# Fused transformer kernel: where in a turn of the first attention the score maxima are taken

## What is computed

```python
def _L0_attn_ref(x, W_Q, W_K, W_V, W_K_prime, W_O, alpha):    # 16 heads of 16, T = 384 rows an image
    scores = jnp.einsum('bhqd,bhkd->bhqk', q, k) / SCALE
    attn = jax.nn.softmax(scores, axis=-1)                     # the row maximum is subtracted
    out_std = jnp.einsum('bhqk,bhkd->bhqd', attn, v)
    scores_p = jnp.einsum('bhqd,bhkd->bhqk', q, kp) / SCALE
    attn_p = jax.nn.softmax(scores_p, axis=-1)
    out_p = jnp.einsum('bhqk,bhkd->bhqd', attn_p, v)
    out = alpha * out_std + (1.0 - alpha) * out_p
...
def fp4_quant_dequant(x):                                      # of w_gate, w_up and w_down too
    scale = jnp.max(jnp.abs(xb), axis=-1, keepdims=True) / 6.0
    scale = jnp.maximum(scale, jnp.float32(1e-12))
    idx = jnp.searchsorted(_MID, jnp.abs(xb / scale))
    q = _GRID[idx] * jnp.sign(xb) * scale
```

## Time and profile before

| | us |
|---|---|
| median of 3 runs | 1869.66 (1868.59 to 1869.83) |
| the profiled execution | 1862.18, its span 1860.4 |
| prologue ring, from about 74.4 | to 135.17, where turn 0 begins |
| turns 0 to 6 | 135.17 to 660.17, 75 on average |
| turn 7, then the wait for the weights | 660.17 to 718.29 |
| PE / DVE / ACT busy over the span | 94% / 54% / 36% |

### The profile page before, as it was taken

The page is one execution under the profiler, slowest core; times in us unless marked ns, Lnnn a source line. Parts: engine busy times, 40 slices in busy tenths (PEclk is TensorE's granted clock), DMA queues, the critical chain, the costliest instruction groups (busy, mean ns, idle before and its releaser), DMA issues. The chain is left out here.

```text
span 1860.4 us, 29106 instructions
## 1 busy us (share of the span) xinstructions
PE 1757.0 (94%) x9935; PEld 1118.6 (60%) x9935; DVE 1007.1 (54%) x2072; ACT 674.2 (36%) x1289; POOL 407.2 (22%) x415
## 2 busy tenths in 40 slices
PE   7989999899999987899989999997999999999997
PEld 3324444344444433677755656655676768999997
DVE  6597877778777877788874554442311111122221
ACT  2116655556566675455432332223111110111110
POOL 2101021120211001788831212110121211100100
PEclk9989999999999999999999999998999999999999
DMA  6832632525425111000056000000010003343311
GB/s 198 132 54 65 91 78 40 99 53 84 78 40 93 25 48 56 17 0 0 1 198 195 1 0 0 0 0 1 18 37 23 30 24 102 124 151 102 105 32 33
DMA packets 111955, 112.84 MB, mean 61 GB/s; under 512 B 11455, under 2 KB 104433, under 8 KB 111858
## 3 DMA queue, kind: packets, MB, share of 16 engines
q1 hardware_dynamic: 98610, 83.21, 20.1%
q10 hardware_dynamic: 9600, 18.92, 2.9%
q0 software_dynamic: 3648, 9.46, 1.4%
HBM read 78.51 MB, written 32.93 MB: 60 GB/s over the span
## 5 line engine op out<-in xcount | busy, mean ns | idle before, releaser
L925 DVE TENSOR_REDUCE mx<-ps_a 128x1 f32<-128x384 f32 x768 | 383.2, 550 | 66.3 <-PE ps_a L567 63.8
L789 ACT ACTIVATE prob<-ps_a 128x768 f32<-128x768 f32 (+1 forms) x512 | 306.2, 650 | 118.7 <-PE ps_a L580 118.6
L567 PE MATMUL ps_a<-w,qs 96*128 96x384 bf16 x768 | 220.1, 338 | 12.3 <-DVE mx L925 5.2
L580 PE MATMUL ps_a<-qs,w 100*128 100x384 bf16 x768 | 208.8, 332 | 6.1 <-issue 3.4
L2090 PEld LDWEIGHTS ps_e<-xTr,w 128*128 128x128 f32 x1792 | 206.1, 193 | 2.2 <-issue 0.8
L2090 PE MATMUL ps_e<-xTr,w 128*128 128x128 f32 x1792 | 206.3, 276 | 0.6 <-DVE xTr L2263 0.6
L567 PEld LDWEIGHTS ps_a<-w,qs 96*128 96x128 bf16 x768 | 61.4, 98 | 180.8 <-DVE mx L925 116.6
L2026 PE MATMUL ps_e<-xT_all,w 128*128 (+1 forms) x512 | 169.3, 490 | 0.9 <-ACT xT_all L2117 0.9
L591 PE MATMUL ps_a<-prob,vp 128*32 128x384 f32 x1536 | 164.1, 500 | 0.0
L2026 PEld LDWEIGHTS ps_e<-xT_all,w 128*128 128x128 f32 x512 | 97.4, 192 | 66.2 <-issue 1.4
L2153 ACT ACTIVATE gel_r<-ps_e 128x512 f32<-128x512 f32 x56 | 33.4, 597 | 280.9 <-PE ps_e L2090 280.9
(11 more groups left out here) (253 smaller groups left out, 2490.2 us busy)
## 6 DMA issues: line engine op xcount, KB each, us to landing
w<-parts_dram SPq DMA_DIRECT2D x192, 96.0 KB, 5.3
w<-in_L_ffn_W_dram ACTq DMA_DIRECT2D x18, 1024.0 KB, 8.3
parts_dram<-w SPq DMA_DIRECT2D x24, 576.0 KB, 3.4
qs<-parts_dram SPq DMA_DIRECT2D x96, 96.0 KB, 4.0
prob<-in_x_dram SPq DMA_DIRECT2D x24, 256.0 KB, 3.6
w<-in_L_ffn_W_dram SPq DMA_DIRECT2D x6, 1024.0 KB, 12.6
grouped_x<-empty_row SPq DMA_DIRECT2D x1, 4352.0 KB, 23.7
grouped_h<-empty_row SPq DMA_DIRECT2D x1, 4240.5 KB, 33.1
```

The source lines that it names most:

```text
L567: mm = pe.matmul(ps[:, r % 3, 0:T], qs[0:NS, b, u // 2, t * P:(t + 1) * P], ks[0:NS, b, u % 2, u // 2], start=True, stop=True)
L580: mm = pe.matmul(ps[:, 4 + t, 0:T], ks[0:NS + 4, b, kp, hh, t * P:(t + 1) * P], qs[0:NS + 4, b, hh], start=True, stop=True)
L789: act.activation(prob[:, g % 2, j, ts.start:ts.stop], ps[:, 4 + ts.start:4 + ts.stop, 0:T], ACT.Exp).then_inc(exp_done.sem, 1)
L925: dve.tensor_reduce(at, ps[:, r % 3, 0:T], AX.X, ALU.max).then_inc(ring_free.sem, 1)
```

## The change

The turn's ring is shifted by 13 units (`OWN`). Units 0 to 12 of turn i now carry entries 58 to 97 of the turn's own image, units 13 to 31 entries 0 to 57 of the next one. The prologue keeps the first 58 entries of image 0, in 29 rounds of two. The last turn gets a ring in its first 13 units, and its 36 weight steps are spread over units 13 to 31. On SP, the second-half maxima of the own image are copied early in the turn, the first-half maxima of the next at its end. On PE a unit's second ring product moves ahead of the values.

```diff
+    OWN = 13
+    HEAD = NR * (UNITS - OWN) // UNITS
     def ring_part(v):
-        return range(NR * v // UNITS, NR * (v + 1) // UNITS)
+        w = (v - OWN) % UNITS
+        return range(NR * w // UNITS, NR * (w + 1) // UNITS)
+
+    def ring_image(i, b, v, more):
+        return (i, b) if v < OWN else (i + 1, 1 - b) if more else None
...
-    EARLY = 3
-    FIRST = -(-NR // EARLY)
+    EARLY = 2
+    FIRST = -(-HEAD // EARLY)
...
                         stacks(i + 1, 1 - b, 1)
-                        maxima(i + 1, 1 - b, 0)
+                    maxima(i, b, 1)
...
                     if more:
-                        maxima(i + 1, 1 - b, 1)
+                        maxima(i + 1, 1 - b, 0)
...
-                for half in range(2):
-                    maxima(0, 0, half)
+                maxima(0, 0, 0)
...
                         scores(i, b, v, 0)
-                        if more:
-                            ring(i + 1, 1 - b, ring_part(v)[:1])
+                        if of_ring:
+                            ring(*of_ring, ring_part(v)[:1])
                         scores(i, b, v, 1)
+                        if of_ring:
+                            ring(*of_ring, ring_part(v)[1:2])
...
-                        if more:
-                            ring(i + 1, 1 - b, ring_part(v)[1:])
+                        if of_ring:
+                            ring(*of_ring, ring_part(v)[2:])
...
-                    n, units = 4 * w4_step.per, UNITS - 9
-                    return range(n * (v - 7) // units, n * (v - 6) // units) if 7 <= v < 7 + units else ()
+                    n, units = 4 * w4_step.per, UNITS - OWN
+                    return range(n * (v - OWN) // units, n * (v - OWN + 1) // units) if v >= OWN else ()
```

More of the change, by code:

```diff
@@ L199, in first_ring @@
     def first_ring(r):
-        return range(r * EARLY, min((r + 1) * EARLY, NR))
+        return range(r * EARLY, min((r + 1) * EARLY, HEAD))
     def edge_piece(r):
@@ L636, in turn @@
                         g, j = v // QUAD, v % QUAD
+                        of_ring = ring_image(i, b, v, more)
                         scores(i, b, v, 0)
-                        if more:
-                            ring(i + 1, 1 - b, ring_part(v)[:1])
+                        if of_ring:
+                            ring(*of_ring, ring_part(v)[:1])
                         scores(i, b, v, 1)
+                        if of_ring:
+                            ring(*of_ring, ring_part(v)[1:2])
                         if j and g:
@@ L1018, in turn @@
                     for v in range(UNITS):
-                        if more:
-                            ring(i + 1, ring_part(v))
+                        of_ring = ring_image(i, b, v, more)
+                        if of_ring:
+                            ring(of_ring[0], ring_part(v))
                         step, n, of = bank3(v, prev, more, more2)
```

## The result

| | before | after |
|---|---|---|
| median of 9 runs each, us | 1868.59 (1862.48 to 1869.88) | 1876.77 (1874.54 to 1880.28) |
| the profiled execution, its span | 1862.18, 1860.4 | 1878.14, 1876.3 |

The account below looks back on a forecast made before the run. Prologue bound by PE and DVE, then DVE; regular turns by PE; the last turn by the chain of weight loads and DVE's 36 steps. -15.5 - 4.3 + 22.8 + 2 = +5.0 on 1869.7 gives 1874.7 us; range 1865.5 to 1881.

Parts of the forecast that it names:

- C: Rival, last turn: the weight loads don't block, so +10.7 us there and no tail cost, 1860.6 us; chance 5%.
- A: Rival, turns 0 to 6: steadily busy DVE wins 2.0 us a turn, -14 in all, 1865.0 us; chance 20%.
- B: Rival, turns' first scores: maxima rows land late, each of seven turns waits 1.0 us, +7, 1881.7 us; chance 15%.
- Part 3: Last turn: weight loads queue on SP behind the maxima copies, so the chain of weight steps starts later; +22.8 us.
- Part 1: Prologue: 58 ring entries in place of 98 make it shorter; -15.5 us, range -17.5 to -12.
- Part 2: Turns 0 to 6: four moved things save about 0.55 us a turn, 1.0 in turn 6; -4.3 us.
- (b): Turns, units without values: the product ahead of the values removes a bank wait; unit 24 keeps 0.3 us.
- (a): Turn's end: no transpose there, so the next turn's first ring product doesn't wait; 0.51 us saved.
- (c): Turns, transposes in units without values: reductions in front are tighter packed, about 0.2 us less than before.
- (d): Unit 12, turns 0 to 5: the transpose waits behind a projection's subtraction and three reductions; about 0.5 us more.
- For a plain unit no change: Turns, plain units: PE has no gap to win and the bank needed earlier is already reduced; no change.
- Part 4: Tail: longer PE idling makes the lower clock likelier when the weights are turned; +2 us, range 0 to +4.

Follow-up runs that it names:

- e1: The changed kernel with the five weight loads issued at the last turn's start, ahead of its row copies; 1866.29 us, ratio 0.9997.
- e4: The kernel before with the weight loads also waiting until the scores of the last turn's first eight units are done; ratio 1.0033.
- e10: The changed kernel once more, unedited, for a second profile; one run, 1879.46 us.
- e3: The changed kernel with both of a unit's later ring products behind the values again; 1884.6 us, ratio 1.0080.
- e5: The kernel before with only a unit's second ring product moved ahead of the values; 1861.02 us, ratio 0.9969.
- e6: e1 with 12 own units in place of 13, so the transposes stand in units 11 and 27; 1857.22 us, ratio 0.9942.
- e2: e1 with 7 own units in place of 13, 76 prologue entries spread evenly over 29 rounds; 1854.61 us, ratio 0.9938.
- e7: e2 with 14 products without use on PE ahead of its wait for the last weight step; 1854.42 us, ratio 0.9929.
- e9: e7 with 8 own units in place of 7; 1854.41 us, ratio 0.9935.
- e8: e2 with 10 own units in place of 7, 67 entries in the prologue; 1857.87 us, ratio 0.9950.

## Point by point: where the prediction held and where not

**The sum.** Predicted 1874.7, measured 1876.77. Against the 1868.59 that before showed beside it, the forecast's +5.0 was +8 to +10 us. The range held the time and the sign was right, but the sum was 3 to 5 us short. That the time itself lies only 2.1 us from the forecast is in part luck: the median of before used for it, 1869.66, was 1.1 us above the later one. (The 17% put outside the range add up to 20: C's 5, half of A's 20, a third of B's 15.) Turn 7's first scores, put at 640.4, came at 650.28: 2.2 of the 9.9 arose ahead of the ring, 2.4 in the prologue, 5.3 in the turns.

**Part 3, the last turn: right.** The maxima were done 25.28 us after the turn's start (24.95 predicted), the first step came 12.3 us later (12.5), at 37.6 (37.4), and the chain took 44.2 (43.4). Its extra 0.8 us lies in one gap of 1.16 us on DVE, waiting for PE's output product at half clock: "without a gap on DVE" didn't hold behind a PE that had idled. +23.8 against +22.8. That loads behind waits on SP are the mechanism is shown from both sides, e1 and e4. The Trainium skill's advice to issue a DMA early (DMA: Bandwidth & Descriptors, Rules for kernel authors) is borne out here at 12.5 us of the last turn. The loads alone are not the loss, though: with them early, in e1, the last turn still takes 11.4 us more than before. Rival C was wrong as put.

**Part 1, the prologue: right in the mean, 2.4 us off in this pair.** -13.1 against -15.5. PE after, then the windows of the edge rounds and of one stretch in them:

```profile
107.69 1.02 PE L673 MATMUL ps_a<-prob 128*128 128x512 f32 x2
...
111.64 1.63 PE L673 MATMUL ps_a<-prob 128*128 128x512 f32 x2
...
118.04 0.31 PE L571 MATMUL ps_a<-ident,mx 128*96 128x128 f32 x1
...
123.06 1.43 PE L574 MATMUL ps_a<-w,qs 96*128 96x384 bf16 x3 [2.04 <-DVE mx L935]
124.31 0.82 PE L587 MATMUL ps_a<-qs,w 100*128 100x384 bf16 x2
```
```profile
94.43:118.04 23.61, 22.21 (x66) 8.56 (x64) 18.42 (x40) 1.58 (x3) 1.66 (x3) 0.93 0.58 102
...
111.90:115.30 3.40, 3.40 (x6) 1.11 (x5) 1.83 (x4) 0.00 (x0) 0.00 (x0) 0.50 0.00 0
```

The reader sees two edge products take 1.63 us at a granted clock of 0.50 (1.2 GHz) where they took 1.02 at 2.4 GHz. The edge rounds were put at 19.7 + 1.0 us and took 23.6, of which 1.7 are this stretch (without it, e10 and e3 have a prologue of 46.0); the rest is 1.2 us of mis-sizing. Rounds 24 to 28 return 0.9 of it, 6.3 us to turn 0's first scores where 8.2 less 1 were put, and rounds 0 to 7 gained 1.0 where 1.3 was taken. Over all profiles the term stands better: the prologue in rounds of three entries took 60.8, 62.2 and 63.9 (before, e4, e5), that in rounds of two 47.7, 47.7, 46.0 and 46.0 (after, e1, e3, e10), means of 62.3 and 46.9: -15.4. The 13.1 came from the shortest of the one and the longest of the other; between those whose edge rounds ran at full clock (before to e10 and e3) it is -14.8.

**Part 2, the turns: the term that failed.** Predicted -4.3, measured +1.0 (and +1.7 between the means of before and e4 and of after, e1 and e10). Three things make up 4.8 to 5.1 of the 5.3; the rest wasn't traced.
- A regular turn won 0.28 in place of 0.55, 1.6 us over six. The step "(b) unit 24 keeps this 0.3" was too small: product and values in the other order win 0.45 (e3 to after), because not only unit 24 gains but other units without values too (the waits for banks in or right behind units 0, 24 and 28 fall by 0.5 in all). The shift, (a), (c) and (d) together, was put at -0.2 and costs +0.17 (before to e3): the transpose of unit 12 waits 1.76 us on PE, 0.8 more than the 0.95 of before, where 0.5 was put, because DVE doesn't only work off the projection's step there but first stands 1.43 us for it (the rows under e6).
- The half clock. Each drop lasts 3.4 us and lengthens its turn by 1.5: turns with one took 77.47 and 77.51 us, the ones beside them 75.95. After had two, 3.1 us. Before had one, in turn 5, which took 76.43 us beside 76.23 for a regular one; without a drop turn 5 is 0.57 shorter than a regular one in after and 0.92 in e5, so it cost before an estimated 0.8 to 1.1. That leaves 2.0 to 2.3 us.
- The turn with the loop's jump cost 5.7 us more than a regular one, before 4.4: 1.2 us. PE's stall at the jump is not the reason, it was shorter (2.5 us, before 3.4); the cause stays open.

"For a plain unit no change" held: no wait appears at the product ahead of the values. I had given the transposes a price in waiting and none in clock. PE in turn 4 after, around unit 12, and the window behind it:

```profile
462.06 0.32 PE L571 MATMUL ps_a<-ident,mx 128*96 128x128 f32 x1 [1.76 <-DVE mx L935]
...
463.88 1.51 PE L598 MATMUL ps_a<-prob,vp 128*32 128x384 f32 x8
```
```profile
463.50:466.90 3.40, 3.40 (x14) 1.19 (x13) 1.95 (x5) 0.83 (x2) 0.59 (x1) 0.50 0.05 10
```

**Part 4, the tail: the number right, the cause only half.** +2.1 against +2. But e4 and e5, with the old last turn, have tails of 18.1 and 18.7 as well. PE at the turning of the weights, e5:

```profile
716.22 3.01 PE L732 MATMUL ps_a<-ident,w 128*128 128x128 f32 x13 [3.00 <-DVE w L1012]
```

Behind the same 3.0 us of idle time as before, 13 products take 3.01 us where before 24 took 2.81. The tail of before was the exception; between means (before, e4, e5 and after, e1, e10) the change costs here 0.9 us (18.7 against 17.7), not 2. That idle time can lower the clock is shown by e2 and e7 above, and the Trainium skill says it too (TensorE: Matmul & The Clock Gate, What's actually happening); that the gap of 3.0 us was harmless, as I read the earlier trace rows, was a reading from one execution.

**The rivals.** A asked for 14 us in the turns; none of the kernels won more than 6.3. B is refuted: no turn's first scores wait for a maxima row, and the own image's row copies hold up PE for 0.5 us, at unit 16 of the last turn. That wait ends at 679.90, 4.3 us behind the maxima and 2.0 behind the start of the last copy's issue, so the landing is near the 2 us at which the prediction had nothing wait, not the 4.

Between the means of the profiles in which a stage's program is the same (for the last turn before and e5, after and e10) the terms are -15.4, +1.7, +24.2 and +0.9, together +11.4; the ratio says +10.3, 7.8 to 12.7. So the turns are the one term that was off by more than this interval leaves open, by 6.0 us; the last turn was 1.4 too low, the tail 1.1 too high.

## What to carry to other kernels

Work shifted out of a prologue comes back in the last turn, and there its price is set by the chain that ends the stage: look at what is queued behind it in written order, a DMA queue included, before counting the work itself. Put a reduction's hand-over in a place where PE has long work to do before it, and not behind a step for which the reducing engine itself has to wait; here one unit's difference, which changed both and took two drops of the clock with it, was worth 6.8 us over seven turns. A difference of 0.3% between two profiled executions can be the clock: take a period at full clock from each, or the mean of several profiles, before pricing a term.

## What the runs showed of the hardware

- Short waits and the clock. In after, e1, e3 and e10, PE waits 1.58 to 1.76 us at the transpose of unit 12 in turns 0 to 5, 24 times in all; half clock begins 0.9 to 1.8 us behind 12 of these. Of the 32 other transposes of turns 0 to 6 in the same four kernels, which wait 1.05 to 1.08, one is followed by a drop (e3, at 615.6); of the 28 in before and e4, which wait 0.95, two; and in e2 and e5 to e9, where none waits over 1.4, there is no drop but at the jump and in turn 0's beginning. So the longer wait makes it likelier, without deciding it; a kernel that changes this wait alone was not run.
- Half clock in a stretch where PE is busy costs about half of its length: 3.4 us of it, 1.5 to 1.7 us of the turn, in turns 1 to 5 without the loop's jump (after, e1, e3, e10).
- PE's issue stall at the loop's jump isn't constant: 2.5 us after, 3.0 e10, 3.2 e7, 3.4 before, 6.5 e9. After and e10 are one kernel, so part of the difference is between executions; how much is between kernels isn't shown.

The version to keep is e2 or e7 (ratios 0.9938 and 0.9929; e9, e6 and e8 aren't told from them): own units few, loads early, one product ahead of the values. It is 12 to 13 us faster than before and 22 to 24 us faster than the changed kernel.
